# A tuned macaron block on one core: expert outputs weighted on VectorE, added to the stream on GpSimd

## The reference

```python
x = x + 0.5 * ffn(layernorm(x))
x = x + attention(layernorm(x), W_qkv, W_out)      # 16 heads of 64, causal
x = x + 0.5 * ffn(layernorm(x))                    # the same weights again
...
gate = x @ Wg.T + routing_bias                      # 8 experts
weights = softmax over the 4 largest gates, 0 for the other experts
out = swiglu(x, Ws1, Ws2, Ws3)                      # the shared expert
eo[e] = (silu(x @ W1[e].T) * (x @ W2[e].T)) @ W3[e].T   # hidden size 341
out = out + sum over e of eo[e] * weights[:, e]
```

## Time and profile before

| | us |
|---|---|
| median of 3 runs | 685.14 (684.83 to 685.91) |
| the profiled execution, first to last instruction | 683.0 |
| PE busy | 646.1 |
| VectorE busy | 609.6 |
| ScalarE busy | 572.8 |
| GpSimd busy | 495.7 |

### The profile page before, as it was taken

One profiled execution on the slowest core, in us unless ns is written; L12 is line 12 of the kernel. 1 busy time (PEld: TensorE's weight loads), 2 busy tenths in 40 slices (PEclk: granted clock), 3 DMA queues, 4 the chain that ended last, 5 costly groups with the idle time before them and its releaser, 6 DMA issues.

```text
span 683.0 us, 20985 instructions
## 1 busy us (share of the span) xinstructions
PE 646.1 (95%) x7846; PEld 414.1 (61%) x7846; DVE 609.6 (89%) x1701; ACT 572.8 (84%) x1110; POOL 495.7 (73%) x589
## 2 busy tenths in 40 slices
PE   5798989999999998999899999999999999999997
PEld 3465755465567565666566566665666567666665
DVE  4899799999998999899889999989999888789887
ACT  6789977898999888899978999997999997565654
POOL 3244775688899687788967889895789898566555
PEclk9999999999999999999999999999999999999999
DMA  7800000278799366588844788683678797100000
GB/s 205 258 1 1 1 2 1 54 111 148 120 129 154 57 104 120 100 140 123 145 75 79 114 140 141 125 137 56 102 125 134 144 144 110 33 1 18 17 2 16
DMA packets 226489, 62.97 MB, mean 92 GB/s; under 512 B 213202, under 2 KB 225620, under 8 KB 226388
## 3 DMA queue, kind: packets, MB, share of 16 engines
q1 hardware_dynamic: 226388, 61.64, 52.4%
HBM read 7.87 MB, written 1.05 MB: 13 GB/s over the span
## 4 chain that ended last, share of the span: by engine, by line
PE 45%; DVE 23%; ACT 16%; issue 9%; POOL 5%; DMA 1%; SPq 0%; ACTq 0%; DVEq 0%; POOLq 0%
PE bank L1068 13%; PE bank L1070 12%; PE bank L1069 12%; ACT probs L1424 6%; DVE probs L1710 4%; DVE glu L1619 3%; DVE xs L1649 3%; ACT glu L1386 3%; PE bank L1238 3%; DVE glu L1624 3%; POOL paired L1035 2%; ACT gluh L1407 2%; PE bank L1201 2%; POOL glul L1031 1%; ACT paired L1432 1%
## 5 line engine op out<-in xcount | busy, mean ns | idle before, releaser
L1031 POOL TENSOR_TENSOR glul<-glu,gluh 128x512 f16<-128x512 f32 x191 | 221.3, 1161 | 98.4 <-ACT gluh L1407 97.9
L1035 POOL TENSOR_TENSOR paired<-probs,paired 128x512 f16<-128x512 f32 x160 | 185.4, 1161 | 27.4 <-ACT paired L1432 24.5
L1386 ACT ACTIVATE glu<-bank,tanh_scale 128x512 f32<-128x512 f32 x167 | 113.3, 678 | 49.1 <-PE bank L1070 48.5
L1619 DVE SCALAR_TENSOR_TENSOR glu<-glu,bank 128x512 f32<-128x512 f32 x167 | 113.7, 681 | 24.8 <-ACT glu L1386 24.4
L1424 ACT ACTIVATE probs<-probs,exp_bias 128x128 f32<-128x128 f32 (+3 forms) x256 | 131.6, 551 | 3.6 <-POOL exp_bias L1043 3.5
L1710 DVE CUSTOM_DVE_ANT_0 probs<-bank,causal,score_scale 128x128 f32<-128x128 f32 (+3 forms) x256 | 128.0, 545 | 6.2 <-POOL paired L1035 5.0
L1068 PE MATMUL bank<-w3h,gluh 128*128 128x128 f16 x708 | 127.4, 220 | 5.9 <-POOL glul L1031 4.9
L1070 PE MATMUL bank<-w3h,glul 128*128 128x128 f16 x708 | 127.2, 220 | 0.0
L1069 PE MATMUL bank<-w3l,gluh 128*128 128x128 f16 x708 | 127.2, 220 | 0.0
L1407 ACT ACTIVATE gluh<-glu 128x512 f16<-128x512 f32 x191 | 118.5, 621 | 2.0 <-DVE glu L1624 2.0
L1624 DVE SCALAR_TENSOR_TENSOR glu<-glu,bank 128x512 f32<-128x512 f32 x167 | 114.7, 687 | 5.8
(11 more groups left out here) (236 smaller groups left out, 1619.8 us busy)
## 6 DMA issues: line engine op xcount, KB each, us to landing
pT<-paired SPq DMA_TRANSPOSE x160, 3.2
attention_raw<-in_L_attn_W_qkv SPq DMA_DIRECT2D x6, 256.0 KB, 5.3
xs<-in_L_attn_inputs SPq DMA_DIRECT2D x4, 256.0 KB, 4.7
vh<-in_L_ffn_W SPq DMA_DIRECT2D x6, 128.0 KB
pT<-in_L_ffn_W SPq DMA_DIRECT2D x6, 128.0 KB
out<-xs SPq DMA_DIRECT2D x3, 256.0 KB, 2.5
raw_more<-in_L_ffn_W SPq DMA_DIRECT2D x4, 128.0 KB
attention_raw<-in_L_attn_W_out SPq DMA_DIRECT2D x2, 256.0 KB, 6.4
```

The lines of the kernel that those rows point to most:

```text
L1031: pool.tensor_tensor(glul[pair][:, :], g[:, :], gluh[pair][:, :], ALU.subtract).then_inc(glu_low)
L1035: pool.tensor_tensor(paired[n % PAIRED][:, 1, :], probs[n % PROBS][:, :], paired[n % PAIRED][:, 0, :], ALU.subtract).then_inc(probs_low)
L1386: act.activation(g[:, :], psum[b1.bank][:, :], ACT.Tanh, scale=tanh_scale[:, j:j + 1]).then_inc(tanh_made)
L1619: v.scalar_tensor_tensor(g[:, :], g[:, :], 1.0, psum[b1.bank][:, :], ALU.add, ALU.mult).then_inc(drained[b1.bank])
```

## The change

All routed experts but the last one of the last layer take another way into the stream. A step `weigh_expert` on DVE multiplies the whole bank (128x512) by the routing weights, repeated over the 128 columns of each token tile, into one of two new SBUF buffers `weighed` (`WEIGHED = 2`); in layer 0 the same instruction also multiplies by `unscale`, and line 1644 is gone. A step `add_up` on POOL adds the buffer to the stream and counts a new semaphore `added_up`. It is put into the list one feed-forward step later, or at once for the layer's last expert and where the second buffer is needed. DVE waits for `added_up` before it writes a buffer that POOL hasn't added yet. The shared expert, which has one scale for all tokens, becomes one instruction of 128x512 that still adds to the stream on DVE. The last expert of the last layer keeps its four instructions; ahead of it POOL must have added all the others. Norms, the attention's output and the stores of the output wait for `added_up` where they waited for `drained`.

```diff
--- before.py
+++ after.py
@@ -103,6 +103,7 @@
 ROUTE_STEP = 0
 SPLIT_LAG = 2
 COLLECT_LAG = 1
+WEIGHED = 2
 STORE_AT = 14
 
 FIRST_NORM = [2, 1, 1]
@@ -138,6 +139,8 @@
 
 Turned = namedtuple("Turned", "n")
 
+Added = namedtuple("Added", "n")
+
 
 class Schedule:
 
@@ -148,7 +151,7 @@
         self.down_uses, self.o_uses, self.summed = {}, [None] * 2, {}
         self.drains, self.fills = [0] * BANKS, [0] * BANKS
         self.splits = self.norms = self.turned_norms = self.tiles = self.parts = 0
-        self.glu_taken = 0
+        self.glu_taken = self.weighed = 0
         self.glu_left = [None] * GLUS
         self.pair_left = [None] * GLU_PAIRS
         self.stream_at = [None] * B
@@ -393,15 +396,31 @@
         tiles, collects, later = {}, [], []
         order = TILE_ORDER if c else range(HT)
         late = {}
+        unadded = []
+
+        def add_up(left=0):
+            while len(unadded) > left:
+                k, use = unadded.pop(0)
+                self.add("add_up", b=b, k=k, use=use, stream=self.stream_at[b])
+                self.stream_at[b] = Added(k + 1)
 
         def collect(i):
             while collects and collects[0][0] < i:
                 _, n, use, done = collects.pop(0)
-                self.add("collect", c=c, b=b, n=n, use=use, done=done, stream=self.stream_at[b])
+                alone = n == 0 or c == 2 * B - 1 and n == NE - 1
+                if alone:
+                    add_up()
+                    self.add("collect", c=c, b=b, n=n, use=use, done=done, stream=self.stream_at[b])
+                    self.stream_at[b] = use
+                else:
+                    add_up(WEIGHED - 1)
+                    self.add("weigh_expert", c=c, n=n, use=use, done=done, k=self.weighed)
+                    unadded.append((self.weighed, use))
+                    self.weighed += 1
                 self.release(use)
                 self.route_left[c % 2] = use
-                self.stream_at[b] = use
                 if n == NE - 1:
+                    add_up()
                     self.finished.add(("ff1" if c < B else "ff2", b))
 
         routing = self.router(c)
@@ -759,6 +779,7 @@
         glul = [sb(f"glul{i}", [P, L], F16) for i in range(GLU_PAIRS)]
 
         qk = [[sb(f"{n}{i}", [P, L], F16) for n in ("qh", "ql", "kh", "kl")] for i in range(2)]
+        weighed = [sb(f"weighed{i}", [P, NT, D]) for i in range(WEIGHED)]
         v_flat = [sb(n, [P, NT * 2 * PAIRS * SUMMED], F16) for n in ("vh", "vl")]
         vh, vl = [v[:, :].rearrange("p (t h d) -> p t h d", t=NT, d=SUMMED) for v in v_flat]
         native_back = sb("native_back", [P, 1])
@@ -800,6 +821,7 @@
         filled = [signal(f"filled{i}") for i in range(BANKS)]
         drained = [signal(f"drained{i}") for i in range(BANKS)]
         down_done = signal("down_done")
+        added_up = signal("added_up")
         pv_done = signal("pv_done")
         high_made = signal("high_made")
         tanh_made = signal("tanh_made")
@@ -926,9 +948,9 @@
                                            attn_pair[gp % 2][:, :, :].rearrange("p a k -> p (a k)")
                                            ).then_inc(heads_turned[gp % TURNED_HEADS], 16)
                 elif kind == "store":
-                    b, use = s["b"], s["stream"]
+                    b = s["b"]
                     if b < B - 1:
-                        q.wait_ge(drained[use.bank], use.n + use.d)
+                        q.wait_ge(added_up, s["stream"].n)
                         sp.dma_start(chunk_of(out, b), xs[:, b * NT:(b + 1) * NT, :]).then_inc(stored, 16)
                     else:
                         for t in range(0, NT, 2):
@@ -1025,6 +1047,15 @@
                         done = pool.tensor_tensor(of, of, unscale[:, 1:NE].unsqueeze(2).broadcast_to([P, E, NT]),
                                                   ALU.mult)
                     done.then_inc(route_made)
+                elif kind == "add_up":
+                    stream, k, use = s["stream"], s["k"], s["use"]
+                    if isinstance(stream, Added):
+                        q.wait_ge(added_up, stream.n)
+                    else:
+                        q.wait_ge(drained[stream.bank], stream.n + stream.d)
+                    q.wait_ge(drained[use.bank], use.n + use.d)
+                    pool.tensor_tensor(stream_of(s["b"]), weighed[k % WEIGHED][:, :, :].rearrange("p t d -> p (t d)"),
+                                       stream_of(s["b"]), ALU.add).then_inc(added_up)
                 elif kind == "split_hidden":
                     g, pair = glu[s["g"]], s["pair"]
                     q.wait_ge(glu_high, s["k"] + 1)
@@ -1463,6 +1494,8 @@
             def stream_ready(b, use):
                 if use is None:
                     q.wait_ge(x_in[b], 16)
+                elif isinstance(use, Added):
+                    q.wait_ge(added_up, use.n)
                 else:
                     q.wait_ge(drained[use.bank], use.n + use.d)
 
@@ -1637,22 +1670,32 @@
                 elif kind == "collect":
                     c, b, n, use = s["c"], s["b"], s["n"], s["use"]
                     stream_ready(b, s["stream"])
-                    if n:
-                        weights = route[c % 2][:, n, :]
-                        q.wait_ge(route_made, c + 1)
-                        if c == 0:
-                            chained(v.tensor_scalar(weights, weights, unscale[:, n:n + 1], None, ALU.mult))
-                            chain()
                     q.wait_ge(down_done, s["done"])
+                    if n == 0:
+                        v.scalar_tensor_tensor(stream_of(b), psum[use.bank][:, :], unscale[:, 0:1], stream_of(b),
+                                               ALU.mult, ALU.add).then_inc(drained[use.bank])
+                        continue
+                    q.wait_ge(route_made, c + 1)
                     for t in range(NT):
                         rows = xs[:, b * NT + t, :]
                         done = v.scalar_tensor_tensor(rows, psum[use.bank][:, t * D:(t + 1) * D],
-                                                      route[c % 2][:, n, t:t + 1] if n else unscale[:, 0:1], rows,
-                                                      ALU.mult, ALU.add)
-                        if c == 2 * B - 1 and n == NE - 1 and t % 2:
+                                                      route[c % 2][:, n, t:t + 1], rows, ALU.mult, ALU.add)
+                        if t % 2:
                             done.then_inc(rows_made)
-                    if c < 2 * B - 1 or n < NE - 1:
-                        done.then_inc(drained[use.bank])
+                elif kind == "weigh_expert":
+                    c, n, use, k = s["c"], s["n"], s["use"], s["k"]
+                    places = psum[use.bank][:, :].rearrange("p (t d) -> p t d", d=D)
+                    weights = route[c % 2][:, n, :].unsqueeze(2).broadcast_to([P, NT, D])
+                    q.wait_ge(route_made, c + 1)
+                    if k >= WEIGHED:
+                        q.wait_ge(added_up, k - WEIGHED + 1)
+                    q.wait_ge(down_done, s["done"])
+                    if c == 0:
+                        v.scalar_tensor_tensor(weighed[k % WEIGHED][:, :, :], places, unscale[:, n:n + 1], weights,
+                                               ALU.mult, ALU.mult).then_inc(drained[use.bank])
+                    else:
+                        v.tensor_tensor(weighed[k % WEIGHED][:, :, :], places, weights, ALU.mult
+                                        ).then_inc(drained[use.bank])
                 elif kind == "add_out":
                     b, use = s["b"], s["use"]
                     stream_ready(b, s["stream"])
```

## The result

The changed kernel takes 702.15 us (701.83 to 702.42, four runs) against 685.12 us before: ratio 1.0249, 95% interval 1.0234 to 1.0263. It is 17 us slower. The forecast was 687.4 us in a range of 679 to 692.5, so the direction came true and the size did not. The time is the one that the prediction gave for "half of the 42.9 us on the path", 702.5 us, and held for too far out. In the sessions of the experiments the kernel before ran between 684.3 and 688.0 us, the longer the lower its mean granted clock (0.995 to 0.990), so differences of less than 2 us between kernels are weak there.

The account below looks back on a forecast made before the run. PE was taken to bound the tail, VectorE to lead narrowly in the middle. Relief -5.5, additions +6.4 and end +1.35 gave +2.25 us on the profiled 683.0; with the median 2.1 us above the span, 687.4 us, range 679 to 692.5.

Parts of the forecast that it names:

- the direction: Whole kernel: slower by 2.25 us, with chances of 0.47 for slower, 0.36 for faster and 0.17 for same.
- half of the 42.9 us on the path: Middle: half of GpSimd's added work reaches the time, +17.3 us in all, 702.5 us; GpSimd as the bound had 0.13.
- those elsewhere at nothing: Additions outside the stretches at 200, 320 and 440 us cost 0, covered by GpSimd's waits or its free tail.
- three stretches of 20 us: At 200, 320 and 440 us GpSimd would need 21.8, 22.0 and 22.6 of 20 us: +6.4 us.
- The second rival: GpSimd becomes the bound of the middle through its queue in the attention: 691.7 or 702.5 us, chance 0.13.
- the case with a quarter: Middle: a quarter of the 42.9 us of additions on the path, +6.6 us in all, 691.7 us, thought nearer.
- The relief of VectorE: Layer 0 and middle: cheaper collects take 9.2 us off the chain, 60% of it counted, -5.5 us.
- the share of the chain times 41%: Collects' chain time, 3.7 us in layer 0 and 14.0 in the middle, of which 41% goes: 1.5 and 5.8 us.
- The end: After PE's last matmul starts: the last collect waits for two GpSimd additions in a row, +1.35 us.
- The added waits: VectorE's waits for `added_up` before it reuses one of two buffers: cost nothing.
- The norm behind layer 0: It reads the stream after GpSimd's last addition, mostly covered by two `glu` products on VectorE: at most 0.5 us.
- The held multiplication: Third rival: GpSimd holds VectorE's new multiplication 0.43 us on average, so VectorE saves nothing: +7.75 us, 692.9 us, chance 0.06.

Follow-up runs that it names:

- e2: The changed kernel with every wait in place, but GpSimd adds only 4 of the 512 columns: 678.59 us, ratio 0.988.
- e11: The changed kernel, but GpSimd adds only the first 256 of the 512 columns: 689.73 us, ratio 1.005.
- e3: The changed kernel, but VectorE does the 63 additions too, at the same steps: 694.13 us, ratio 1.012.
- e1: The kernel before with only the shared expert added in one VectorE instruction of 128x512 instead of four: 686.65 us, ratio 1.0008.
- e9: The changed kernel with additions on GpSimd only in layers 1 to 5, routed experts elsewhere collected as before: 699.46 us, ratio 1.019.
- e7: The changed kernel with additions on GpSimd in layer 0 alone, routed experts elsewhere collected as before: 687.88 us, ratio 1.002.
- e17: The kernel before with six buffers of softmax probabilities and the norm's two small instructions on GpSimd: 689.86 us, ratio 1.006.

## Why the prediction was wrong

- **The direction and the mechanism.** Slower, by GpSimd's work in the attention: right. The direction was held for no more than likely, 0.47 against 0.36 for faster. That GpSimd would become as full as ScalarE on average was right too, 427 of 485 us.
- **The step that failed** is "those elsewhere at nothing". The prediction charged the additions only in three stretches of 20 us in which GpSimd's work would have come to more than 20 us, +6.4 us, and let its waits for ScalarE cover the others. Measured, the additions cost 23.6 us by the medians, 24.0 by the traces from 45 us on. The three stretches have 4.4 of it (0.2, 2.1 and 2.1 us), about what was charged. The rest, put at nothing, is the other stretches of the middle with 13.7 us, layer 0 with 3.2 and the tail with 1.1; 1.6 are the end. So the error is the criterion: that a stretch of GpSimd with room in it takes an addition for free. It did in nine stretches with 18 additions and didn't in others, also where GpSimd was busy 13.8 of 20 us. A likely reason, argued and not shown for single places: ScalarE, GpSimd and PE hand the same tiles on, so an addition that fills a wait can still stand ahead of the next low half. On average over the 39 additions of the middle it came to 0.46 us each.
- **The weight of the rivals.** The second rival had the right mechanism and, with half of the additions on the path, 702.5 us. It was given 0.13, and the case with a quarter was thought nearer. That its number fits to 0.4 us is luck in part: it has 21.5 us for the middle, where 18.1 were measured, and nothing for layer 0 and the tail, where there were 4.3 or more. The chain gave GpSimd 5% before, and the prediction took a small share of the chain for a small price at the margin, while the sum of three engines, all over 80% busy in the middle and in the same order of hand-overs, spoke against it.
- **The relief of VectorE.** Forecast -5.5 us, measured -7.0 (e2), or about -5 without the 2.1 us at the half clock of the kernel before. Right in kind, and the share of the chain times 41% was a usable estimate.
- **The end.** Forecast +1.35, measured 1.6 between the marks and the span; the addition's 1277 ns in place of 1161 explain 0.23 of it.
- **The added waits** for the buffers: nothing, right (e2). The norm behind layer 0 was put at 0.5 us at most, and that was too little: its place costs 1.4 us, the sum's wait and the longer `var_eps` together. **The held multiplication**: didn't happen. But other VectorE instructions were held, for 10 us of busy time, which no step of the prediction had, though its own row of line 1644 at 1.17 us was such a one.

## What to carry to other kernels

From this one kernel, where several engines pass the same tiles round in a fixed order and three of them are over 80% busy: don't take an engine with idle time, or a stretch of it, for an engine with room. Here work added to GpSimd cost about a third of its length over the whole, between nothing and nearly all of it in single places, and the busy time of the place didn't tell which. Measure it by occupying that engine with idle work in an otherwise unchanged kernel. The exchange of 0.43 us less on VectorE for 1.28 us more on GpSimd lost on balance beside attention, and also in layer 0, where GpSimd was little over half busy. In the tail, in which PE alone sets the pace, it cost less than a tenth of a microsecond for each addition. And before a gain in one stretch of a trace is put down to an edit, look at the granted clock there in both traces.

## What the runs showed of the hardware

- GpSimd's f32 addition of 128x512 takes 1277 ns, its subtraction of f16 from f32 with an f16 result 1163; the addition of 128x256 in f32 takes 731 (e11). VectorE's f32 addition of 128x512 out of SBUF takes 999 ns (e3), its product of a PSUM bank with a repeated SBUF operand 682.
- A `tensor_scalar` of 128x4 on VectorE lasted up to 2.65 us, until there was a gap in GpSimd's work; in the changed kernel such instructions took 6.3 us over twelve `neg_mean` and 5.2 over twelve `var_eps`; in e2, with the same instructions and GpSimd less busy, 3.5 and 1.9. VectorE's products with a PSUM operand kept their length to within 2 ns (683 against 681).
- TensorE's granted clock fell to 0.50 in short stretches, in the kernel before from 274.0 to 277.4 us (PE had been busy 2.0 of the 4.0 us before), in the changed kernel from 90.6 to 94.0 (1.8 of 4.0). One such stretch at about 92, 274 or 552 us shifts all that follows by 1.1 to 2.2 us (e1 and e9; e2 against before; e7 and e17).
